# A graph layer with routed experts: unfilled blocks carried on, tile 0 routed like the others, pairs earlier, down product ahead of up

## Time and profile before

| | |
|---|---|
| median of 3 runs | 2856.91 us (2855.78 to 2860.61) |
| the profiled execution's own time | 2839.81 us |
| its span in the trace | 2837.9 us, 38299 instructions |
| granted TensorE clock, mean | 0.826 |
| PE, PEld, DVE, ACT, POOL busy | 75%, 52%, 56%, 39%, 51% |
| DMA queue 0 (POOL's) and 1 (SP's), share of 16 engines | 26.9%, 20.3% |

### The profile page before, as it was taken

How to read it: one execution, slowest core, us unless ns; L and a number is a source line. 1 busy time by engine, 2 the same in 40 slices (tenths; PEclk the granted TensorE clock), 3 DMA queues, 4 the chain that set the end, 5 groups by cost and what they waited for, 6 DMA issues and landing times.

```text
span 2837.9 us, 38299 instructions
## 1 busy us (share of the span) xinstructions
PE 2122.6 (75%) x9465; PEld 1477.9 (52%) x9466; DVE 1593.9 (56%) x3892; ACT 1094.5 (39%) x1977; POOL 1454.0 (51%) x1584
## 2 busy tenths in 40 slices
PE   8578887667767777667678778778777787687887
PEld 6346665445555555444445545555554464455545
DVE  6656666556666665765545546555554454375531
ACT  5322222234443442434344455455333333154532
POOL 3465556666666666543445555555555655431311
PEclk9788997777777767777789888988888898887899
DMA  9644444755554555444544554445454544454431
GB/s 304 143 124 127 124 122 115 251 150 154 148 147 145 153 141 151 126 143 136 152 138 139 148 138 136 140 139 149 135 141 134 145 139 133 110 153 137 124 91 45
DMA packets 292093, 402.38 MB, mean 142 GB/s; under 512 B 113059, under 2 KB 214723, under 8 KB 288366
## 3 DMA queue, kind: packets, MB, share of 16 engines
q0 software_dynamic: 74112, 205.81, 26.9%
q1 hardware_dynamic: 199724, 170.47, 20.3%
q10 hardware_dynamic: 18034, 23.56, 2.8%
HBM read 346.13 MB, written 82.22 MB: 151 GB/s over the span
## 4 chain that ended last, share of the span: by engine, by line
PE 21%; another core or an unknown queue 8%; ACT 8%; issue 8%; ACTq 4%; DVE 1%; DVEq 0%
PE psC L2363 6%; PE psD L2414 4%; PE psB L2322 4%; PE psA L2496 1%; ACT acc L2222 1%; ACTq L2178 1%; ACT local_row L2101 1%; ACT acc L2236 1%; ACTq L2177 1%; ACT hid L2137 1%; ACTq L2176 1%; PE psC L2360 1%; PE psC L2384 1%; ACT acc L2225 1%
## 5 line engine op out<-in xcount | busy, mean ns | idle before, releaser
L1516 POOL DMA_INDIRECT rows_g<-node_table,src_all x1347 | 1284.7, 954 | 993.7 <-PE psB L2322 424.2
L2322 PE MATMUL psB<-rows_g,pick_e 128*128 128x260 f32 x2704 | 762.6, 439 | 121.1 <-issue 115.7
L2322 PEld LDWEIGHTS psB<-rows_g,pick_e 128*128 128x128 f32 x2704 | 584.3, 222 | 254.4 <-issue 153.0
L2105 ACT ACTIVATE pick_n<-local_row 128x1024 bf16<-128x1024 bf16 x169 | 178.6, 1057 | 722.2 <-remote 479.9
L1690 DVE TENSOR_TENSOR rows_g<-rows_g,psD 128x2048 f32<-128x2048 f32 x169 | 384.8, 2277 | 0.0
L2363 PE MATMUL psC<-W_f,xnT 128*128 x468 | 322.7, 827 | 0.0
L2414 PE MATMUL psD<-W_f,hidT 128*128 x936 | 254.4, 418 | 0.0
L1753 DVE COPY xn<-psD 128x256 f32<-128x256 f32 x117 | 49.5, 423 | 362.8 <-PE psD L2414 143.9
L1537 POOL DMA_INDIRECT rows_g<-set_dram,places x96 | 93.3, 972 | 278.2 <-issue 168.4
L2101 ACT ACTIVATE local_row<-local_row,minus_id 128x1024 bf16<-128x1024 bf16 x169 | 191.9, 1136 | 63.9 <-issue 54.8
L2414 PEld LDWEIGHTS psD<-W_f,hidT 128*128 128x128 f32 x936 | 184.1, 208 | 41.1 <-issue 8.9
(11 more groups left out here) (389 smaller groups left out, 3078.6 us busy)
## 6 DMA issues: line engine op xcount, KB each, us to landing
local_row<-local_dram SPq DMA_DIRECT2D x169, 256.0 KB
rows_g<-node_table,src_all POOLq DMA_INDIRECT x1347
xin<-sent_dram SPq DMA_DIRECT2D x117, 128.0 KB
set_dram<-xn SPq DMA_DIRECT2D x117, 128.0 KB
xnT<-in_xT_dram SPq DMA_DIRECT2D x96, 128.0 KB
sent_dram<-sorted_dram SPq DMA_DIRECT2D x92, 128.0 KB
sent_dram<-sorted_dram ACTq DMA_DIRECT2D x92, 128.0 KB
acc<-node_table SPq DMA_DIRECT2D x49, 128.0 KB
```

The costliest lines, as they stand in the source:

```text
L1516: pool.indirect_dma_start(out=rows_g[:, r, j], out_offset=None, in_=node_table, in_offset=bass.IndirectOffsetOnAxis(ap=src_all[:, g, j:j + ...
L2105: act.activation(pick_n[:], local_row[:, r], ACT.Relu, bias=1.0, scale=-1.0).then_inc(pick_n_ready, 1)
L2322: last = pe.matmul(ps_sum[s % 2][:, 0:AW], pick_e[:, s % SLOTS, j], rows_g[:, s % RING, j, 0:AW], start=(j == 0), stop=(j == EG - 1))
```

## The change

- **Unfilled blocks carried on.** Four sets (48-24, 23-10, 9-4, 3-0). Only sets 2 and 3 are *closed*, that is, filled up. Sets 0 and 1 give only as many blocks as are full for certain, and what remains of each expert stays for the next set. Sets 0 to 2 share one block file and form one span. `fills` runs for closed sets alone, at the later of the table's step and ten steps after the route of the set's last tile but one.
- **Tile 0 sorted too.** It belongs to set 3, is sorted, handed out and collected like the others; the dense jobs, their weights and their stores go.
- **Pairs** start seven steps after the last `spread` (step 143 in place of 169).
- **Collecting.** All tiles but the last set's from five steps after the last block of set 2, three a step.
- **PE's order**: down before up, for blocks.
- `counts_of` is laid out the other way round: `(a d)` in place of `(d a)`. The counts of the routing are in bf16 (`both`, `after`, `seen_half`, `ones_half`).
- `table` keeps begin and shift of each set of a span; `relocate` is done once per span, in chunks of 16 tiles, two steps apart, with one comparison per set.

```diff
-CUTS = (24, 7)
+CUTS = (24, 10, 4)
+CLOSED = (2, 3)
 TAIL_RATE = 3
-COLLECT_RATE = 2
+COLLECT_RATE = 3
...
-    SETS = tuple(zip((FULL,) + tuple(c - 1 for c in CUTS), CUTS + (1,)))
+    SETS = tuple(zip((FULL,) + tuple(c - 1 for c in CUTS), CUTS + (0,)))
+    spans = tuple(zip((0,) + tuple(x + 1 for x in CLOSED[:-1]), CLOSED))
...
-                pair_at = [NS + k for k in range(PAIRS)]
+                pair_at = [spread_at[-1] + 7 + k for k in range(PAIRS)]
-    set_blocks = [(2 * sum(P if t < FULL else TAIL for t in range(lo, hi + 1)) + NE * (P - 1)) // P for hi, lo in SETS]
+    for z, (_, lo) in enumerate(SETS):
+        first = spans[span_of[z]][0]
+        routed = 2 * sum(P if t < FULL else TAIL for t in range(lo, SETS[first][0] + 1))
+        set_at.append(sum(set_blocks[first:z]))
+        set_blocks.append((routed + NE * (P - 1)) // P - set_at[z] if z in CLOSED else -(-(routed - NE * (P - 1)) // P) - set_at[z])
...
-    SORTED = tuple(range(SETS[0][1] - 1, 0, -1))
+    SORTED = tuple(range(SETS[0][1] - 1, -1, -1))
...
-    at = max(max(job_at) + 1, route_at[0] + 3)
-    for e in range(NE):
-        job_at[at + e] = (len(job_step), "dense", e, 0)
-        job_step[len(job_step)] = at + e
...
+    others = [t for w in range(len(SETS) - 1) for t in tiles_in[w]]
+    for f, t in enumerate(others):
+        final_at[t] = job_step[last_job[-2]] + 5 + f // COLLECT_RATE
...
+    reloc_at = {}
+    for w, (_, z) in enumerate(spans):
+        for c, a in enumerate(range(SETS[z][1], SETS[spans[w][0]][0] + 1, P // NE)):
+            reloc_at[table_at[z] + 6 + 2 * c] = (z, a, min(P // NE, SETS[spans[w][0]][0] + 1 - a))
...
-            counts_of = cells(counts_at, P * NT // 2).bitcast(I16).rearrange("p (d a) -> p d a", a=NT)
+            counts_of = cells(counts_at, P * NT // 2).bitcast(I16).rearrange("p (a d) -> p d a", a=NT)
...
-                    sp.wait_ge(fills_out, 16 * NE * (x + (1 if t == SETS[x][1] else 0)))
+                    if filled_by(x if t == SETS[x][1] else x - 1):
+                        sp.wait_ge(fills_out, filled_by(x if t == SETS[x][1] else x - 1))
...
-                        for x in range(len(SETS)):
-                            if table_at[x] == c:
+                        for x in CLOSED:
+                            if max(table_at[x], route_at[SETS[x][1] + 1] + 10) == c:
                                 fills(x)
...
-                    then(dve.tensor_scalar(end_i[:, 0], pos[:], float(P - 1), None, ALU.add))
+                    then(dve.tensor_scalar(end_i[:, 0], pos[:], float(P - 1) if x in CLOSED else 0.0, None, ALU.add))
...
+                    else:
+                        then(dve.tensor_scalar(taken, blk_end[:], -1.0, float(nb), ALU.mult, ALU.add))
+                        then(dve.scalar_tensor_tensor(out=taken, in0=taken, scalar=0.0, in1=blocks[:], op0=ALU.max, op1=ALU.min))
+                        then(dve.tensor_tensor(end_f[:], begin[:, 0:NE], taken, ALU.add))
...
+                def relocate(x, a, tiles, at):
...
+                    for z in range(x + 1 - spans[span_of[x]][0]):
+                        then(dve.tensor_tensor(past, was.unsqueeze(2).broadcast_to([P, 2 * tiles, NE]), every(starts[:, :, z]), ALU.is_ge))
+                        then(dve.tensor_tensor(past, past, every(shift[:, :, z]), ALU.mult))
+                        then(dve.tensor_reduce(by if z == 0 else by_more[:, 0:2 * tiles], past, AX_X, ALU.add))
+                        if z:
+                            then(dve.tensor_tensor(by, by, by_more[:, 0:2 * tiles], ALU.add))
...
-                        if jobs_with(s):
+                        if jobs_with(s) and jobs_with(s)[1] == "mix":
                             up(*jobs_with(s))
                         small_free(s)
                         if jobs_with(s - 2):
                             down(*jobs_with(s - 2))
+                        if jobs_with(s) and jobs_with(s)[1] != "mix":
+                            up(*jobs_with(s))
                         for t in range(FULL, -1, -1):
                             if route_at[t] + 3 == s:
                                 logits(t)
-                            if route_at[t] + 4 == s and t:
+                            if route_at[t] + 4 == s:
                                 count(t)
...
-                    pe.matmul(ps_small[0:rows, count_at], ones_all[:, 0:rows], seen[:], start=False, stop=True).then_inc(counted, 1)
+                    pe.matmul(ps_small[0:rows, count_at], ones_half[:, 0:rows], seen_half[:], start=False, stop=True).then_inc(counted, 1)
```

More of the change, by code:

```diff
@@ L1151, in loop_stage @@
             y_tile0 = cells(5120, D)
-            hidden_cols = cells(5800, NE * HK).rearrange("p (e c) -> p e c", c=HK)
-            n_dense = min(n for n in job_step if job_at[job_step[n]][1] == "dense")
+            spare_cells = lambda v: cells(5760 - 80 + 24 * v, NE * SPAN_MAX)
+            moves, starts, shift = (spare_cells(v).rearrange("p (e x) -> p e x", x=SPAN_MAX) for v in range(3))
+            moves_row, shift_row = spare_cells(0), spare_cells(2)
+            taken = cells(5960, NE)
+            by_more = cells(5960 + NE, 2 * P // NE)
+            assert SPAN_MAX == 3
             ex, ex1 = cells(5376, NT), cells(5376 + NT, NT)
@@ L1462, in on_sync @@
                         job = jobs_with(c - 3)
-                        if job and job[1] != "dense":
+                        if job:
                             store(*job)
@@ L1745, in result @@
                     u = n % 2
-                    if n >= 2 and kind != "dense":
+                    if n >= 2:
                         dve.wait_ge(ys_out[u], stored(u, n - 2))
@@ new lines, in table @@
+                    if x == 0:
+                        then(dve.tensor_tensor(filled, pos[:], region[:], ALU.add))
+                    z = x - spans[span_of[x]][0]
+                    then(dve.scalar_tensor_tensor(out=starts[:, :, z], in0=begin[:, 0:NE], scalar=float(P), in1=region[:], op0=ALU.mult, op1=ALU.add))
+                    then(dve.tensor_scalar(blk_end[:], blk_end[:], float(set_at[x]), float(P), ALU.add, ALU.mult))
+                    then(dve.tensor_tensor(moves[:, :, z], blk_end[:], starts[:, :, z], ALU.subtract))
@@ L1898, in relocate @@
+                def relocate(x, a, tiles, at):
                     for u in range(3):
                         dve.wait_ge(sent[u], 32 * scattered(u))
-                    dve.wait_ge(place_i_ready, route_number(lo) + 1)
-                    dve.wait_ge(xd_ready, sum(1 for t in route_at if route_at[t] + 2 < table_at[x] + 6))
-                    for a in range(lo, hi + 1, P // NE):
-                        tiles = min(P // NE, hi + 1 - a)
-                        pairs = places[:, a:a + tiles].rearrange("p t c -> p (t c)")
-                        was, by = was_all[:, 0:2 * tiles], by_all[:, 0:2 * tiles]
-                        past = scratch[:, 0:2 * tiles * NE].rearrange("p (c e) -> p c e", e=NE)
-                        every = lambda row: row[:].unsqueeze(1).broadcast_to([P, 2 * tiles, NE])
-                        then(dve.tensor_copy(was, pairs))
-                        then(dve.tensor_tensor(past, was.unsqueeze(2).broadcast_to([P, 2 * tiles, NE]), every(region), ALU.is_ge))
-                        then(dve.tensor_tensor(past, past, every(shift), ALU.mult))
-                        then(dve.tensor_reduce(by, past, AX_X, ALU.add))
-                        last = dve.tensor_tensor(pairs, was, by, ALU.add)
-                        if a + tiles <= hi:
-                            then(last)
@@ L1915, in relocate @@
-                    last.then_inc(relocated, 1)
+                    dve.wait_ge(place_i_ready, route_number(SETS[x][1]) + 1)
+                    dve.wait_ge(xd_ready, sum(1 for t in route_at if route_at[t] + 2 <= at))
+                    pairs = places[:, a:a + tiles].rearrange("p t c -> p (t c)")
+                    was, by = was_all[:, 0:2 * tiles], by_all[:, 0:2 * tiles]
+                    past = scratch[:, 0:2 * tiles * NE].rearrange("p (c e) -> p c e", e=NE)
+                    every = lambda row: row.unsqueeze(1).broadcast_to([P, 2 * tiles, NE])
@@ new lines, in relocate @@
+                    then(dve.tensor_copy(was, pairs))
+                    for z in range(x + 1 - spans[span_of[x]][0]):
[4 more added lines that the diff above has]
+                            then(dve.tensor_tensor(by, by, by_more[:, 0:2 * tiles], ALU.add))
@@ L1917, in shares @@
+                    dve.tensor_tensor(pairs, was, by, ALU.add).then_inc(relocated, 1)
                 def shares(x):
-                    hi, lo = (0, 0) if x == len(SETS) else SETS[x]
+                    hi, lo = SETS[x]
                     cols = slice(lo, hi + 1)
@@ L2266, in on_scalar @@
                             take_x(jobs_with(s + 1)[0])
-                        if jobs_with(s - 2) and jobs_with(s - 2)[1] != "dense":
+                        if jobs_with(s - 2):
                             take_h(*jobs_with(s - 2))
```

171 lines of the change are left out of this document (54 added, 117 removed).

## The result

The changed kernel took 2839.22 us (median of 4 runs, 2831.46 to 2839.52) beside 2857.98 for the kernel before (4 runs): ratio 0.9937, interval 0.9911 to 0.9963, or 19 us less. The forecast was 41 us less. The sign and the range hold, the size does not, and in the other condition that the experiments met the sign turned: it held by luck.

A forecast was written before the change was run, and what follows sets the result against it. No engine was full; PE, busy 75% of the span, was taken as nearest its limit in the loop, its order ending the later steps. +70 - 81 - 25 - 5 = -41 us took 2856.9 to 2816 us, range about 2790 to 2845.

The forecast's parts named there:

- The tail: From the last loop step's end on PE to the end: 289 us against 370, so -81 us.
- (a): PE's stall after the loop: tile 2's hand-out stays, the pair's preparation goes; 10 us left (0 to 20).
- (b): After the loop, 19 steps of a block each, 6.8 us instead of 7.6 with down first: 129 us.
- (c): After the loop, a new wait: the last set's fills, with tile 0's hand-out behind them; +25 us (10 to 40).
- (d): From step 188 POOL collects the 43 tiles left, two gathers each at 1.25 us, then the end: 125 us (115 to 160).
- rival B: Collects behind the last block do not keep up, 10 us per three tiles for 7.5: +36, 2852 us; chance 0.12.
- Down before up: Block steps: PE runs down while it waited for gelu; -25 us (0 to -52), from waits in the loop.
- The small edits: Extra table and relocation, missing blocks, bf16 counts, strided piece writes, dropped first-set fills: together -5 us (-25 to +20).
- my +8: Pieces now write with a stride: 0.2 to 0.4 us more on each of 54 operations, half hidden: +8 us.
- The pairs: Pairs move into 25 steps of the edge loop, at 2.8 us a step: +70 us (+35 to +130).
- +10 for the relocation: In pair steps, one more table and a relocation of 45 tiles, about 13 us of DVE: +10 us.
- Rival A: Pairs tie DVE and PE together: product, weights, product in a row, 5.5 us x 25 = 137, 2883 us; chance 0.18.

The follow-up runs named there:

- after_again: The changed kernel, unchanged, timed and profiled again beside the kernel before on a faster chip: 2355.24 us beside 2320.03, ratio 1.0159.
- faster condition: The three other chips of the experiments, where the kernel before, unchanged, ran in 2315 to 2320 us in place of 2857.
- first condition: The chip condition of the first measurement: the kernel before 2857.98 us, the changed kernel 2839.22 us, ratio 0.9937.

## Why the prediction was half right

**The tail, forecast -81, measured -91.6 (first) and -90.7 (faster).** Right, and its parts nearly so. From the last loop step's end on PE (2467.97 in the earlier trace rows, 2558.5 here) to the end it is 279 us where the text had 289. (a) The 10 us at the loop's end did not come. (b) The undisturbed block steps take 5.9 us, not 6.8, and 6.4 with up first: the 7.6 from which I took 0.8 was a mean with disturbed steps in it, and those stay disturbed. (c) The fills and hand-outs in the tail cost what was expected. SP's fills and ACT's hand-out stand in a row in the timeline of the changed kernel:

```profile
2630.94 0.26 PE L2379 MATMUL psD<-acc 24*128 24x256 bf16 x1 [2.94 <-ACT hidT L2127]
...
2633.62 9.81 SPq L1422 DMA_DIRECT2D sent_dram<-zero_dram  x8
...
2647.01 6.12 ACTq L2162 DMA_DIRECT2D sent_dram<-sorted_dram  x4
2653.23 0.39 ACT L2110 ACTIVATE xnT<-psA 128x256 f32<-128x256 f32 x1 [21.94 <-DMA sent_dram<-sorted_dram]
...
2654.24 0.37 PE L2379 MATMUL psD<-acc 24*128 24x256 bf16 x1 [16.64 <-ACT hidT L2127]
```

PE stood 16.6 us there and 2.9 at the hand-out before: 20 of the 25. (d) The collects kept up. POOL's group for 2541 to 2838, which answers to L1537 in the earlier trace rows:

```profile
L1541 POOL DMA_INDIRECT rows_g<-set_dram,places x98 | 96.1, 980 | 206.9 <-issue 181.6 <-DVE rows_g L1943 14.0 <-DMA set_dram<-xn 9.8
```

It waited 14 us for L1943 where the same wait had been 102, and rival B is out. In this trace 38 of the 98 gathers overlap a two-operand combine. 27 of them took 0.94 to 0.99 us, much like the rest, and 11 took 1.0 to 1.2, some 2 us in all; of the 60 others only the first two took more than 0.96. The prediction's "beside them and without them" was no test: in the kernel before only 2 of 96 such gathers overlap a combine. The Trainium skill (SBUF — State Buffer, "Who interferes with whom") has the loser blocked for the whole instruction; the trace shows a delay of at most 0.23 us beside combines of 0.48, not on every gather.

**Down before up, forecast -25.** The total of 25 us on the kernel before and 24 on the changed one, both in the faster condition, agrees with this number by luck. The forecast had the tail's part, 19 steps at 0.8 = 15 us, in (b) already, and its -25 was for the waits in the loop. There the part is worth 8 to 10 us. The forecast for the reorder as a whole was 40, and 24 to 25 came.

**The small edits, forecast -5.** Steps 76 to 82, where the fills of the first set had stood, are 10.8 us shorter in the first condition, 0.4 in the faster. The adds of pieces are the missed size: I took 0.2 to 0.4 us each from the cost of a strided **read**, and they now write with a stride too: 1609 ns for 515 of the earlier trace rows, 42 us of DVE in all. On the path it cost 7 to 9 us (699.7 to 692.8, and 702.1 to 693.1), since DVE had room in these steps: my +8 met that by luck, from a wrong size and a wrong share. What the bf16 counts and the table were worth was not measured apart.

**The pairs, forecast +70.** This is the step that failed: "I take 2.8 x 25 = +70". Measured 98 us, 3.9 a step, in the first condition, and 139, 5.6 a step, in the faster one. That is the whole of these steps, for which I had also put +10 for the relocation and -6 for the missing blocks. The step summed each engine's own work (2.35, 3.5, 3.2 us) and asked which engine sets the pace. None did. The greater part of the price was the order on DVE's queue: the weights of pair k+1 were put ahead of the keep of pair k. The edit that reorders them and removes no work takes the price in the faster condition to 1.7 us a step (286.3 - 243.2 = 43 us in 25 steps), below my 2.8 and near its low end of 1.4 (35 / 25).

Rival A had the kind of mechanism, a tie between engines, and its price of 5.5 us a step, which the faster condition met. It named the product and the weights in a row, but not the place: DVE stood not at its first operation (L1671, here L1675, of which the wait list of the pair steps in `after_again` has no wait) but at the weights, for ACT. Nor did it say that an order and not a need made the tie. I gave it 0.18 on the argument that the pieces are tied the same way and their steps take 14.8 us. The pair steps took 17.1. The argument left out that a piece's add waits behind no work of ACT for the next piece.

**Why the sign was luck.** The order that the reader can see in the code costs 94 us in the faster condition. The pairs cost 98 us in the first condition and 139 in the faster one, and these 41 us are most of the 54 between a win of 19 and a loss of 35. In the first condition an edge step without pairs is already 13.2 us long instead of 9.7; I take it that part of the chain lies there beside waits that stand anyway, which no run shows. The forecast had neither the chain nor its slack. In the first condition its errors made up for each other in part: 24 us too few in the pair steps (98 beside 70 + 10 - 6) and, by the measure of the faster condition, about 15 too many for the reorder in the loop, against 10 too few for the tail. With these three, -41 becomes -12 where -19 was measured.

## What to carry to other kernels

When a stage moves under a loop, do not add up the engines' work alone. Write down each in-order queue's sequence for one step with the semaphore that each entry waits for, and look for an entry that waits for another engine ahead of an entry on which the next iteration hangs; place work for the next step behind it. Time a change beside the old kernel on more than one chip when the old kernel has slack whose cause you don't know: here the same change was worth +1.6% on one chip and -0.6% on another.

## What the runs showed of the hardware

**Two levels of the whole kernel.** On the three chips of the experiments the kernel before was 19% shorter, with DVE busy 1589 us against 1594, ACT 1095 in both, POOL 1454 in both. PE was busy 1929 us against 2123, at a mean granted clock of 0.898 against 0.826. The waits differ too. ACT's pick on the page of the changed kernel in the first condition:

```profile
L2104 ACT ACTIVATE pick_n<-local_row 128x1024 bf16<-128x1024 bf16 x169 | 178.6, 1057 | 634.2 <-remote 451.9
```

and in the faster one:

```profile
L2104 ACT ACTIVATE pick_n<-local_row 128x1024 bf16<-128x1024 bf16 x169 | 178.6, 1057 | 338.0 <-PE psA L2293 315.5
```

In the first one, 452 us of ACT's waits end with something that the trace cannot name, and the profile gives no landing time for the local_row loads; in the faster one such a load lands after 3.7 us and the waits end with PE. My expectations called the first condition one of late transfers. That was a guess, and this wait speaks against it. By the program L2104 waits for its own L2100 (which alone waits for the load) and for PE's pick L2293. In the pair step above, L2100 ended at 2216.31 and the pick at 2217.55, and L2104 began 4.2 us after that:

```profile
2215.18 1.13 ACT L2100 ACTIVATE local_row<-local_row,minus_id 128x1024 bf16<-128x1024 bf16 x1
...
2221.77 1.06 ACT L2104 ACTIVATE pick_n<-local_row 128x1024 bf16<-128x1024 bf16 x1 [5.46 <-remote]
```

No run shows the cause of the first condition, and it stays open.

**The clock follows the stalls.** In the same 25 steps the granted clock was 0.99 without pairs, 0.88 with the tied pairs and 0.95 with the weights moved, means over stretches that lie between the lower level (1.2 GHz) and the upper (2.4 GHz), nearest the upper without pairs. In the tied steps of `after_again` PE's pick stood for the keep 14 times, up to 9.2 us, 47.9 in all. From 1916.4 to 1930.2 PE was busy 4.7 of 13.8 us at a mean granted clock of 0.85, the last 9.2 of them without a matmul; from 1930.2 to 1933 the clock was 0.50, the lower level, and the 16 sums behind took 5.4 us:

```profile
1930.26 0.37 PE L2293 MATMUL psA<-window,pick_n 128*128 128x24 bf16 x8 [9.21 <-DVE acc L1595]
...
1933.03 5.40 PE L2304 MATMUL psB<-rows_g,pick_e 128*128 128x260 f32 x16 [1.03 <-issue]
```

Behind the pair steps, at a granted clock of 1.00, they take:

```profile
2086.59 3.67 PE L2304 MATMUL psB<-rows_g,pick_e 128*128 128x260 f32 x16
```

A record of these sums takes 382 ns at the least and 773 at the most in both kernels, and the median is 383 and 382, so the 26 us by which they got shorter with the move (123.9 to 98.3) are records that no longer ran at the lower clock. Up to 26 of the 96 us that the move took off the pair steps are therefore clock: here a stall cost more than its own length.

**A stride on DVE.** A read of int16 at 98 bytes from one another adds 1.1 ns an element ((491 - 347) / 128). Reading and writing int16 at 256 bytes adds 3.7 ns an element ((1609 - 515) / 294, and the same for the narrowest, (675 - 311) / 98). The Trainium skill (SBUF — State Buffer, "Door 1: The DMA port swizzle") says that an access that crosses to a new line of 16 bytes pays a penalty. The trace agrees in kind: 98 and 256 bytes both leave the line at every element; if a read at 256 bytes costs what one at 98 does, the write side is 2.6 of the 3.7 ns, an estimate, since no run has the write alone.
